# A depthwise 5x5 filter on 128 images: in four tiles of each channel, one product for the high and the low part of the taps

## What is computed

```python
k = jnp.transpose(kernel, (1, 2, 0))[:, :, None, :]
y = lax.conv_general_dilated(x, k, window_strides=(1, 1), padding='SAME',
        dimension_numbers=('NHWC', 'HWIO', 'NHWC'), feature_group_count=ch)
return x + y
```

## Time and profile before

| | |
|---|---|
| Median of 3 runs | 820.39 us (820.22 to 821.93) |
| Profiled execution, its own time | 820.37 us |
| Its span, first to last instruction | 818.6 us |
| TensorE busy | 805.5 us, 98% |
| DVE busy | 690.1 us, 84% |
| ACT busy | 624.1 us, 76% |
| POOL busy | 525.6 us, 64% |
| DMA | 304.43 MB, mean 372 GB/s |

### The profile page before, as it was taken

One profiled execution on the slowest core, in us unless ns is written; L12 is line 12 of the kernel. 1 busy time (PEld: TensorE's weight loads), 2 busy tenths in 40 slices (PEclk: granted clock), 3 DMA queues, 4 the chain that ended last, 5 costly groups with the idle time before them and its releaser, 6 DMA issues.

```text
span 818.6 us, 19135 instructions
## 1 busy us (share of the span) xinstructions
PE 805.5 (98%) x6912; PEld 805.4 (98%) x6912; DVE 690.1 (84%) x1828; ACT 624.1 (76%) x1442; POOL 525.6 (64%) x652
## 2 busy tenths in 40 slices
PE   5999999999999999999999999999999999999997
PEld 5999999999999999999999999999999999999997
DVE  6898888888888888888888888888888888888885
ACT  5777878787777778787777778787777777787775
POOL 7858566576665675756748566576565674756741
PEclk9999999999999999999999999999999999999999
DMA  9999999999999999999999999999999999999965
GB/s 357 426 426 408 375 381 363 383 368 385 368 370 389 364 381 376 375 381 364 378 377 379 386 368 370 377 376 378 382 361 382 372 386 376 368 376 376 381 261 229
DMA packets 28749, 304.43 MB, mean 372 GB/s; under 512 B 3184, under 2 KB 3312, under 8 KB 4208
## 3 DMA queue, kind: packets, MB, share of 16 engines
q1 hardware_dynamic: 28656, 303.22, 97.1%
HBM read 153.79 MB, written 149.42 MB: 370 GB/s over the span
## 4 chain that ended last, share of the span: by engine, by line
PE 98%; POOL 1%; DMA 0%; issue 0%; DVE 0%; ACT 0%; DVEq 0%
PE sums L380 33%; PE sums L383 33%; PE sums L382 33%; DMA first<-consts 0%; POOL matrix L263 0%; POOL spread L250 0%; POOL spare L238 0%; POOL taps L241 0%; POOL taps L236 0%; DVE y_out L333 0%; ACT y_out L292 0%; DVEq L132 0%
## 5 line engine op out<-in xcount | busy, mean ns | idle before, releaser
L380 PE MATMUL sums<-matrix,x_low 126*128 126x208 f32 (+5 forms) x2304 | 648.1, 281 | 8.3 <-POOL matrix L263 8.3
L383 PE MATMUL sums<-matrix,x_high 126*128 126x208 f32 (+5 forms) x2304 | 647.3, 281 | 0.0
L382 PE MATMUL sums<-matrix,x_high 126*128 126x208 f32 (+5 forms) x2304 | 646.3, 281 | 0.0
L292 ACT ACTIVATE y_out<-sums 128x270 f32<-128x270 f32 (+6 forms) x1152 | 443.4, 392 | 183.3 <-PE sums L383 179.5
L263 POOL TENSOR_TENSOR matrix<-spread,mask 127x300 fp32r<-127x300 f32 x384 | 338.5, 913 | 262.3 <-PE sums L383 262.1
L380 PEld LDWEIGHTS sums<-matrix,x_low 126*128 126x128 f32 (+1 forms) x2304 | 443.9, 193 | 8.2 <-POOL matrix L263 8.2
L383 PEld LDWEIGHTS sums<-matrix,x_high 126*128 126x128 f32 (+1 forms) x2304 | 444.3, 193 | 0.0
L382 PEld LDWEIGHTS sums<-matrix,x_high 126*128 126x128 f32 (+1 forms) x2304 | 444.2, 193 | 0.0
L333 DVE TENSOR_TENSOR y_out<-sums,y_out 128x120 f32<-128x120 f32 (+3 forms) x1344 | 295.5, 255 | 117.7 <-ACT y_out L292 113.8
L323 DVE TENSOR_TENSOR x_low<-x_in,x_high 128x768 fp32r<-128x768 f32 x384 | 379.8, 989 | 2.0 <-ACT x_high L285 2.0
L285 ACT ACTIVATE x_high<-x_in 128x768 fp32r<-128x768 f32 x288 | 239.8, 833 | 6.0 <-DMA x_in<-x 5.8
(11 more groups left out here) (4 smaller groups left out, 0.4 us busy)
## 6 DMA issues: line engine op xcount, KB each, us to landing
x_in<-x SPq DMA_DIRECT2D x95, 1536.0 KB, 9.9
y<-y_out SPq DMA_DIRECT2D x95, 1520.0 KB, 12.9
rest<-later SPq DMA_DIRECT2D x1, 2300.0 KB, 14.4
x_in<-x SPq DMA_DIRECT2D x4, 384.0 KB, 5.5
y<-y_out SPq DMA_DIRECT2D x1, 832.5 KB, 3.4
y<-y_out SPq DMA_DIRECT2D x1, 687.5 KB, 4.0
mask<-masks SPq DMA_DIRECT2D x1, 300.0 KB, 3.7
first<-consts SPq DMA_DIRECT2D x1, 125.0 KB, 2.1
```

The costliest lines, as they stand in the source:

```text
L292: act.activation(outputs(c, rows, cols), sums(c, t, rows, cols), ACT.Copy).then_inc(copied, 1)
L380: pe.matmul(target, low, turned[HIGH], start=tile is bank["tiles"][0], stop=False, skip_group_check=True)
L382: pe.matmul(target, high, turned[LOW], start=False, stop=False, skip_group_check=True)
L383: product = pe.matmul(target, high, turned[HIGH], start=False, stop=last, skip_group_check=True)
```

## The change

In the corner tile of the four corner banks, the two products that have the high part of x as stationary operand become one. It moves both parts of the taps, 2 x 11 x 16 = 352 columns, and writes them to different places of the bank: the high sums where they were, the low sums into 16 further columns at the right of the plane, whose pitch there becomes 46 instead of 30 (11 x 46 = 506 of the bank's 512 words). The first product, low x by high taps, stays as it was. A channel has 68 products.

The low sums are then added to `y_out` by DVE, with a further add of 128 x 176 behind the seams of banks 0, 5, 8 and 9: 18 adds a channel. By the plan, the corners of banks 5 and 8 wait for their own bank's seam, and bank 1's seam for the corner of bank 0. Bank 10's two adds change places and wait for bank 9's seam and corner; bank 11's third add waits for bank 10's first. Bank 0, which had no add, is now released by DVE. Copies, seams, splits, the cast and the order of all else are the same.

```diff
+CORNERS = ((0, 0), (2, 0), (2, 1), (0, 1))
+SPAN = 2 * LONG + HALO
+EDGE = LONG + HALO
...
-            banks.append(dict(quarter=quarter, kind=kind, rows=rows, cols=cols, tiles=tiles,
-                              deep=short[1] - short[0], pitch=long[1] - long[0]))
+            row, k = CORNERS[quarter]
+            corner = k if n == row else None
+            banks.append(dict(quarter=quarter, kind=kind, rows=rows, cols=cols, tiles=tiles, corner=corner,
+                              deep=short[1] - short[0], pitch=SPAN + EDGE * (corner is not None)))
+            if corner is not None:
+                across_it = tuple(long[0] + w for w in tiles[corner]["wide"])
+                banks[-1]["corner_cells"] = (rows, across_it) if kind == FLAT else (across_it, cols)
...
-            bank["adds"].append((seam, after[-1] if after else 0))
+            bank["adds"].append((seam, after[-1] if after else 0, HIGH))
             earlier.append(seam)
+        if bank["corner"] is not None:
+            cells_of_corner = bank["corner_cells"]
+            after = [n + 1 for n, e in enumerate(earlier) if meet(e, cells_of_corner)]
+            bank["adds"].append((cells_of_corner, after[-1] if after else 0, LOW))
+            earlier.append(cells_of_corner)
...
+        def low_sums(c, t):
+            plane = plane_of(c, t)[:, :, SPAN:SPAN + EDGE]
+            return plane.rearrange("p x y -> p y x") if PLAN[t]["kind"] == TALL else plane
+
+        def both_sums(window, wide):
+
+            return bass.AP(tensor=window.tensor, offset=window.offset,
+                           ap=[window.ap[0], [SPAN - wide[0], 2], window.ap[1], window.ap[2]])
...
-                    dve.tensor_tensor(y, sums(c, t, rows, cols), y, ALU.add).then_inc(added, 1)
+                    terms = sums(c, t, rows, cols) if part == HIGH else low_sums(c, t)
+                    dve.tensor_tensor(y, terms, y, ALU.add).then_inc(added, 1)
...
-                        pe.matmul(target, low, turned[HIGH], start=tile is bank["tiles"][0], stop=False,
+                        pe.matmul(target, low, turned[:, HIGH], start=tile is bank["tiles"][0], stop=False,
                                   skip_group_check=True)
-                        pe.matmul(target, high, turned[LOW], start=False, stop=False, skip_group_check=True)
-                        product = pe.matmul(target, high, turned[HIGH], start=False, stop=last, skip_group_check=True)
+                        if bank["corner"] is not None and tile is bank["tiles"][bank["corner"]]:
+                            product = pe.matmul(both_sums(target, wide), high, turned, start=False, stop=last,
+                                                skip_group_check=True)
+                        else:
+                            pe.matmul(target, high, turned[:, LOW], start=False, stop=False, skip_group_check=True)
+                            product = pe.matmul(target, high, turned[:, HIGH], start=False, stop=last,
+                                                skip_group_check=True)
```

More of the change, by code:

```diff
@@ L326, in add_seams @@
             def add_seams(c, t):
-                for n, ((rows, cols), after) in enumerate(PLAN[t]["adds"]):
+                for n, ((rows, cols), after, part) in enumerate(PLAN[t]["adds"]):
                     if n == 0:
@@ L375, in _ @@
                         high, low = x_high[c % SLOTS][0:pixels, images], x_low[c % SLOTS][0:pixels, images]
-                        turned = [matrix[c % SLOTS][kind][0:pixels, part, :].rearrange("p (r q) -> p r q", q=COLS)[
-                            :, tile["from_row"]:tile["from_row"] + deep,
-                            tile["from_col"]:tile["from_col"] + wide[1] - wide[0]] for part in (HIGH, LOW)]
+                        turned = matrix[c % SLOTS][kind][0:pixels, :, :].rearrange("p h (r q) -> p h r q", q=COLS)[
+                            :, :, tile["from_row"]:tile["from_row"] + deep,
+                            tile["from_col"]:tile["from_col"] + wide[1] - wide[0]]
                         last = tile is bank["tiles"][-1]
-                        pe.matmul(target, low, turned[HIGH], start=tile is bank["tiles"][0], stop=False,
+                        pe.matmul(target, low, turned[:, HIGH], start=tile is bank["tiles"][0], stop=False,
                                   skip_group_check=True)
-                        pe.matmul(target, high, turned[LOW], start=False, stop=False, skip_group_check=True)
-                        product = pe.matmul(target, high, turned[HIGH], start=False, stop=last, skip_group_check=True)
+                        if bank["corner"] is not None and tile is bank["tiles"][bank["corner"]]:
[5 more added lines that the diff above has]
+                                                skip_group_check=True)
                     product.then_inc(sums_done, 1)
```

## The result

The changed kernel takes **858.3 us** (857.9 to 858.8, 4 runs), the one before 820.5: a ratio of 1.046, interval 1.044 to 1.048. The forecast was 810.7 us, range 804 to 822. It was wrong in sign.

What follows compares the result with a forecast made beforehand. The prediction took TensorE's products to bound the kernel, with DVE's added work covered by idle time and the cast. Saving 0.10 us in each of 95 channels, 9.7 us, from 820.39 gave 810.7 us, range 804 to 822.

Steps and rivals of the forecast that it cites:

- TensorE's part: Merging two products in four corner tiles per channel was to save TensorE 0.10 us a channel.
- the row price: On TensorE, rows and not width set a product's time: 9.2 ns a row, 8.2 at most in quarters 2 and 3.
- The rule by columns: The Trainium skill's price for an isolated TensorE product, columns divided by 2.4 ns plus 2.5: 0.149 us for 352 columns.
- its rival: On TensorE, columns set the merged product, at 0.128 to 0.179 us; kernel at 800 or 806 us; chance 0.09.
- the sum: TensorE's saving per channel, 2 x 0.018 + 2 x 0.032 = 0.10 us, with DVE's added work covered.
- The four adds: DVE's new corner adds of 128 x 176: 0.25 us each, 1.00 a channel, or 0.33 each if tails do not overlap.
- three waits: DVE adds waiting for the add just issued, at banks 0, 5 and 8: 0.12 us each, 0.36 a channel.
- Does DVE hold?: DVE's balance per channel: 1.36 us added against 1.38 of room; with TensorE's channel 0.10 shorter, 0.08 short, so DVE full.
- give: DVE's cast, started a few tenths later, was to end at the same time behind POOL's products, covering up to 0.4 us.
- DVE takes the bound: Rival: DVE sets the channel from the split of piece 0 to the next cast; 826 us, chance 0.23 wholly or partly.
- What moves: Bank 0's release about 2.5 us into the channel, bank 11's adds 1 us later, SP's loads and stores up to 1 us.

Runs made afterwards that it cites:

- the products alone: The changed kernel with DVE's four adds of the low sums left out and the merged products kept: 804.9 us, ratio 0.981.

## Why the prediction was wrong

*TensorE's part was right for the merged product, and left out the product behind it.* Products in the changed kernel, from start to start:

```profile
359.31 0.27 PE L403 MATMUL sums<-matrix,x_low 126*128 126x176 f32 x1
359.41 0.38 PE L406 MATMUL sums<-matrix,x_high 126*128 126x352 f32 x1
359.63 0.27 PE L403 MATMUL sums<-matrix,x_low 126*128 126x198 f32 x1
...
359.95 0.29 PE L403 MATMUL sums<-matrix,x_low 126*128 126x208 f32 x1
...
362.98 0.37 PE L406 MATMUL sums<-matrix,x_high 126*128 126x352 f32 x1
363.18 0.27 PE L403 MATMUL sums<-matrix,x_low 126*128 126x198 f32 x1
...
363.40 0.27 PE L410 MATMUL sums<-matrix,x_high 126*128 126x198 f32 x1
364.02 0.35 PE L403 MATMUL sums<-matrix,x_low 126*128 126x234 f32 x1 [0.35 <-DVE y_out L356]
...
365.90 0.35 PE L406 MATMUL sums<-matrix,x_high 126*128 126x352 f32 x1
366.10 0.26 PE L403 MATMUL sums<-matrix,x_low 126*128 126x198 f32 x1
...
368.08 0.27 PE L403 MATMUL sums<-matrix,x_low 126*128 126x176 f32 x1
```

The merged product takes 0.22, 0.20 and 0.20 where the row price gave 0.202, 0.202 and 0.181. The rule by columns, 0.149, does not hold here, and its rival, which went up to 0.179, falls with it; that the rival's 806 us lies near the 804.9 of the products alone is luck. Bank 0's six products took 0.67, its five now 0.64.

The saving is nevertheless 0.164 and not 0.10. Means over 80 channels, of the kernel before and of the one with the products alone, show where it is: the four merged products save 0.083, near the 0.10 of the sum, and the products directly behind them, which the sum had unchanged, save another 0.091; the rest takes 0.01 more. Bank 10's first product, behind bank 9's corner, took 0.14 before (from 460.84 to the first row here) and takes 0.11 with the products alone (the other two rows):

```profile
460.98 0.28 PE L382 MATMUL sums<-matrix,x_high 126*128 126x234 f32 x1
```

```profile
345.47 0.28 PE L400 MATMUL sums<-matrix,x_low 126*128 126x234 f32 x1
345.58 0.28 PE L406 MATMUL sums<-matrix,x_high 126*128 126x234 f32 x1
```

Why a product is shorter behind a merged one stays open.

*The four adds:* sized right. The *three waits* nearly: 0.12 was taken. From the changed kernel, a seam, its corner and the subtraction behind it, then bank 0's corner and bank 1's seam:

```profile
437.11 0.28 DVE L356 TENSOR_TENSOR y_out<-sums,y_out 128x120 f32<-128x120 f32 x1
...
437.42 0.34 DVE L356 TENSOR_TENSOR y_out<-sums,y_out 128x176 f32<-128x176 f32 x1
437.68 0.95 DVE L345 TENSOR_TENSOR x_low<-x_in,x_high 128x768 fp32r<-128x768 f32 x1
...
443.35 0.33 DVE L356 TENSOR_TENSOR y_out<-sums,y_out 128x176 f32<-128x176 f32 x1
...
443.78 0.28 DVE L356 TENSOR_TENSOR y_out<-sums,y_out 128x120 f32<-128x120 f32 x1
```

The corner takes 0.26 for 0.25. From the seam to its corner it is 0.31 as forecast, so 0.12 each at banks 5 and 8; at bank 0, where the next add waits for two counters, 0.43 instead of 0.25, so 0.18. In all 0.42 for 0.36.

*"Does DVE hold?" is the step that failed.* It put 0.99 of corners and waits in front of the last adds and left every subtraction at its old duration. But three corners and two waits also stand in front of the subtraction of piece 3, whose end lay at the start of POOL's products, 462.55. The step itself used the fact that decides: it read off that the cast ends 0.41 after POOL's products, and booked that as "give". The same turn-taking holds for the subtractions, and there it is a charge, for which the sum had no term. With the measured terms: 6.98 without idle time and tails, corners 1.00, waits 0.42, subtractions 0.75, cast -0.30, together 8.85; the timeline has 368.08 - 359.31 = 8.77, so the terms account for it within 0.08. The forecast had 8.34. TensorE's rows show the consequence: it stops at bank 6 (363.40 to 364.02, 0.62 for 0.11), whose place in PSUM bank 10's adds of the channel before must empty, and those now come behind the late subtraction of piece 3. The channel is 0.51 longer than the 8.26 forecast, 95 x 0.51 = 48 us, which is the whole difference between 810.7 and 858.3.

*The rival "DVE takes the bound"* named the right engine and place, with a chance of 0.23 and 826 us. Its argument against itself, that a DVE that lags moves its cast out of POOL's products, came true (0.92 to 0.62) and was outweighed: the lag moved two subtractions into them.

*What moves:* bank 0's release, stores and loads cost nothing, as said, though not all stores were down in time: ACT waited for one 24 times, 20.3 us in all (once and 2.2 before). None of this reached the bound, since DVE's waits for ACT are 0.9 us in all. Bank 11's and bank 10's adds did not come "1 us later" but as late as TensorE's wait allows.

## What to carry to other kernels

When an engine has little room left, adding work costs more than the work: what stands behind it in the list is moved, and must be laid against what the neighbour does at the new moment. A price read at one place of the schedule (0.99 for a subtraction) holds only there; if one instruction of an engine is seen to wait for another engine's instruction to end, ask it of every instruction of that kind. And small changes of order (corners behind the subtraction, or not directly behind the add that they need) can be worth more than the work itself: here 53 us, and the version so ordered, at 804.9, beats both kernels.

## What the runs showed of the hardware

- A DVE subtraction with both inputs in SBUF and a POOL product exclude each other, instruction by instruction. The one that comes second waits for the rest of the other's; both orders are seen above (DVE waits at 438.92, POOL at 439.49). A subtraction that finds a product in progress ends 0.81 to 0.82 us after it. The Trainium skill's rule, in the section named above, has this pair contend, and the trace agrees: 1.43 instead of 0.95 at 438.92.
- An add that waits for the add just ahead costs 0.12 us, and 0.18 in the one place where it waits for another counter as well; that the second counter is the reason was not tried. "VectorE: DVE Perf Modes" of the Trainium skill, section "The DRAIN you can't avoid", has a semaphore after each of eight copies cost nothing; here the measurement differs.
- The time of a product with short rows goes by its rows here: 13 rows took 0.120 us with 208 columns and with 234, 9.2 ns a row, and the merged products' 22 rows of 16 took 0.20 to 0.22, 9 to 10 ns a row.
